# A graph layer and an eight-expert layer on one core: the last two token groups in an order of their own, and expert tiles that wait for fewer rows

## What is computed

```python
h = layernorm(x)                                   # (8, 1024, 128)
agg = eps * h + adj @ h                            # adj (8, 1024, 1024)
h = silu(rmsnorm(agg @ W1 + b1) * rms_weight)      # 512 wide
x = x + h @ W2 + b2
z = layernorm(x)
scores = z @ Wg.T + bg                             # 8 experts
top2, probs = top_k(scores, 2), softmax over the two
x = x + sum over the two: prob * (relu(z @ F1[e].T + fb1[e]) @ F2[e].T + fb2[e])
```

## Time and profile before

| | us |
|---|---|
| median of three runs | 699.27 (698.19 to 699.67) |
| the profiled execution | 698.98 |
| its span | 697.2 |
| PE busy | 591.9 (85%) |
| POOL busy | 385.1 (55%) |
| DVE busy | 453.2 (65%) |
| ACT busy | 359.3 (52%) |

### The profile page before, as it was taken

The page is one execution under the profiler, slowest core; times in us unless marked ns, Lnnn a source line. Parts: engine busy times, 40 slices in busy tenths (PEclk is TensorE's granted clock), DMA queues, the critical chain, the costliest instruction groups (busy, mean ns, idle before and its releaser), DMA issues.

```text
span 697.2 us, 13635 instructions
## 1 busy us (share of the span) xinstructions
PE 591.9 (85%) x4143; PEld 544.5 (78%) x4143; DVE 453.2 (65%) x1389; ACT 359.3 (52%) x852; POOL 385.1 (55%) x473
## 2 busy tenths in 40 slices
PE   1789899999989999999865499999999999999400
PEld 1668787878878787888754399999999999999400
DVE  2457989888898988888745345555454554555173
ACT  3257585866757586675542244444544445454200
POOL 4233268767676876767575236556555555556500
PEclk9889999999999999999995599999999999999855
DMA  7962344332444432245412655556555555563099
GB/s 262 324 184 116 121 153 148 124 111 80 147 152 153 149 114 111 90 146 153 153 39 79 205 206 191 197 183 216 181 195 195 172 204 189 185 206 126 3 398 323
DMA packets 59760, 116.49 MB, mean 167 GB/s; under 512 B 8399, under 2 KB 35072, under 8 KB 59688
## 3 DMA queue, kind: packets, MB, share of 16 engines
q1 hardware_dynamic: 50792, 98.62, 41.8%
q0 software_dynamic: 8896, 17.00, 7.2%
HBM read 61.80 MB, written 25.63 MB: 125 GB/s over the span
## 4 chain that ended last, share of the span: by engine, by line
PE 64%; DVE 12%; ACT 9%; issue 5%; DMA 4%; POOL 3%; SPq 1%; POOLq 0%; DVEq 0%; ACTq 0%
PE ps_y L628 10%; PE ps_g L628 9%; PE ps_agg L462 6%; PE ps_agg L464 5%; PE ps_agg L463 5%; PE ps_t L469 5%; PE ps_y L576 4%; PE ps_h L462 4%; PE ps_h L463 4%; PE ps_h L464 4%; DVE adjT_lo L943 3%; ACT adjT_hi L664 3%; DMA adj_in<-parts 3%; DVE hn L1026 3%; PE ps_t L605 2%
## 5 line engine op out<-in xcount | busy, mean ns | idle before, releaser
L902 POOL DMA_INDIRECT parts<-adj_in,goes x150 | 145.7, 971 | 125.7 <-ACT adj_in L781 60.1
L852 POOL DMA_INDIRECT slots<-rows,dest x128 | 128.5, 1004 | 43.5 <-issue 38.3
L781 ACT ACTIVATE adj_in<-adj_in,share 128x128 f32<-128x128 f32 x150 | 49.4, 392 | 134.8 <-issue 123.0
L943 DVE TENSOR_TENSOR adjT_lo<-ps_t,adjT_hi 128x512 fp32r<-128x512 f32 x128 | 88.1, 689 | 34.0 <-ACT adjT_hi L664 31.0
L664 ACT ACTIVATE adjT_hi<-ps_t 128x512 fp32r<-128x512 f32 x128 | 76.1, 596 | 63.5 <-PE ps_t L469 63.3
L469 PE MATMUL ps_t<-ident,adj_in 128*128 128x128 f32 x512 | 79.8, 281 | 13.2 <-POOL adj_in L838 13.2
L469 PEld LDWEIGHTS ps_t<-ident,adj_in 128*128 128x128 f32 x512 | 66.5, 146 | 31.1 <-issue 14.4
L462 PE MATMUL ps_agg<-adjT_hi,xn_hi 128*128 128x512 f32 (+1 forms) x152 | 69.9, 460 | 10.5 <-DVE adjT_lo L943 10.5
L1128 DVE CAST goes<-adj_in 128x3 int32<-128x3 f32 x50 | 9.6, 192 | 103.7 <-DMA parts<-adj_in,goes 94.3
L628 PE MATMUL ps_g<-W2e,hn 128*128 x600 | 71.0, 275 | 0.0
L628 PE MATMUL ps_y<-W2e,hb 128*128 x600 | 71.0, 275 | 0.0
(11 more groups left out here) (176 smaller groups left out, 1317.8 us busy)
## 6 DMA issues: line engine op xcount, KB each, us to landing
adj_in<-in_adj SPq DMA_DIRECT2D x16, 2048.0 KB, 10.0
W1cur<-W1e SPq DMA_DIRECT2D x26, 512.0 KB, 3.1
adj_in<-slots SPq DMA_DIRECT2D x50, 196.5 KB, 2.5
xn_hi<-W1e SPq DMA_DIRECT2D x12, 512.0 KB, 3.1
xn_lo<-W1e SPq DMA_DIRECT2D x12, 512.0 KB, 3.1
W1e<-parts SPq DMA_DIRECT2D x4, 1024.0 KB, 8.2
adj_in<-parts SPq DMA_DIRECT2D x4, 1024.0 KB, 16.0
out<-x_all SPq DMA_DIRECT2D x8, 512.0 KB, 6.2
```

The source lines that it names most:

```text
L781: ins = act.activation(ye[ku][:, j, :], yb[ku % 2][:, j, :], ACT.Copy, scale=share[ku][:, j:j + 1])
L852: pool.indirect_dma_start(out=slots, out_offset=bass.IndirectOffsetOnAxis(ap=dest[1 - par][:, c, j:j + 1], axis=0), in_=rows[1 - par][:, c ...
L902: pool.indirect_dma_start(out=parts, out_offset=bass.IndirectOffsetOnAxis(ap=goes[ku][:, j:j + 1], axis=0), in_=ye[ku][:, j, :], in_offset ...
L943: dve.tensor_tensor(adjT_lo[m % 2][:, :], ps_t[m % 2][:, :], adjT_hi[m % 2][:, :].bitcast(FP32), ALU.subtract).then_inc(s_lo, 1)
```

## The change

**Steps 0 to 15 are as before.** Behind them groups 14 and 15 (q - 1 and q, with q = 15) have a list of their own on every engine:

- PE: all four products of `first_layer` for group 15 into four banks (`h_last`), with no expert weights between them; the transposes of the hidden layer with those of group 14's normed rows (now into `ps_t[0]`) between; the second layer of group 15 with group 14's gate inside it; group 14's ranks; `expert_weights` 0 to 3; normed rows and gate of group 15; `expert_weights` 4 to 6; group 15's ranks; `expert_weights` 7. The weights now rotate over three pairs of banks (`w_bank`), so expert e waits for the copies of expert e - 2 or e - 3.
- DVE, ACT and POOL have lists that go with it. On POOL the scatter of group 13 is split around the two inverse square roots, and group 15's inverse square root stands ahead of all of group 14's scatters.
- `fill_tails` moves from SP to ACT, behind all copies of weights and ahead of ACT's first work on tiles.
- SP loads the rows of tile 0 ahead of its weights, and rows 0, 1 and 2 (`AHEAD` = 3) wait for all even groups, but for the odd groups and the paddings only up to numbers read from `enough`. DVE works those out behind `table`: if expert 0 has at least 896 + 384 t rows, then tile t lies in rows that group 15 cannot reach, and 896 (all odd groups but 15) and the 7 spare paddings are enough; if not, everything is waited for. Rows 3 wait for everything.
- DVE makes `low_weights` 5 to 7 behind the table and not within it. POOL makes three more constants at the start (`sure` and the two halves of `fewest`).

```diff
+    AHEAD = 3
+    ENOUGH = (16 * GT * (NG - 2), 16 * SPARE)
+        h_last = (ps_h[0], ps_h[1], ps_agg[0], ps_agg[1])
+
+        def w_bank(e, i):
+
+            return (ps_t, ps_agg, ps_h)[e % 3][i]
...
@@ sync
-            sp.wait_ge(s_tail, 1)
-            fill_tails(sp, range(E))
             sp.wait_ge(s_table, 1)
-            sp.wait_ge(s_wTa, 2 * E)
-            sp.wait_ge(s_wTd, E)
-            sp.wait_ge(s_fb1c, 1)
-            sp.wait_ge(s_fb2, 16)
+            sp.wait_ge(s_late, 1)
...
+                if t < AHEAD:
+                    rows_in, pads_in = [sp.value_load(enough[0:1, i, t:t + 1], min_val=ENOUGH[i], max_val=ENOUGH[i] + 128)
+                                        for i in range(2)]
+                    sp.wait_ge(s_scat[0], 16 * GT * NG)
+                    sp.wait_ge(s_scat[1], rows_in)
+                    sp.wait_ge(s_pads, pads_in)
+                elif t == AHEAD:
+                    sp.wait_ge(s_scat[1], 16 * GT * NG)
+                    sp.wait_ge(s_pads, 16 * (SPARE + E))
...
+            load_rows(0, 0)
+            sp.wait_ge(s_wTa, 2 * E)
+            sp.wait_ge(s_wTd, E)
+            sp.wait_ge(s_fb1c, 1)
+            sp.wait_ge(s_fb2, 16)
             load_weights(0, 0)
-            sp.wait_ge(s_tails, 16 * E)
-            sp.wait_ge(s_spare, 16 * SPARE)
-            sp.wait_ge(s_scat[0], 16 * GT * NG)
-            sp.wait_ge(s_scat[1], 16 * GT * NG)
-            load_rows(0, 0)
...
@@ tensor
-            first_part(pe, step, NG + 1)
+            first_part(pe, step, NG - 1)
+
+            q = NG - 1
+            pe.wait_ge(s_agg, NG)
+            first_layer(q, range(GT), h_last)
+            pe.wait_ge(s_hn, NG)
+            pe.wait_ge(s_hna, NG)
+            transpose_hidden(q, (0, 1))
+            pe.wait_ge(s_lo, TPB * NG)
+            transpose_normed(q - 1, ps_t[0])
+            transpose_hidden(q, (2, 3))
+            second_layer(q, (0,))
+            gate(q - 1)
+            second_layer(q, (1, 2, 3))
+            rank(q - 1)
+            for e in range(4):
+                expert_weights(e)
+            transpose_normed(q, ps_y)
+            gate(q)
+            for e in range(4, 7):
+                expert_weights(e)
+            rank(q)
+            expert_weights(7)
...
@@ scalar
+            for e in range(4):
+                copy_weights(e)
+            normed(q, ps_y)
+            second_rows(q)
+            for e in range(4, E):
+                copy_weights(e)
+            act.wait_ge(s_tail, 1)
+            fill_tails(act, range(E))
...
@@ gpsimd
+            scatter_rows(q - 2, 0)
+            rms_factors(q)
+            ln2_factors(q - 1)
+            scatter_rows(q - 2, 1)
+            ln2_factors(q)
+            pool.wait_ge(s_dest, q)
+            pool.wait_ge(s_row2, q)
+            for c in range(2):
+                scatter_rows(q - 1, c)
+            pool.wait_ge(s_dest, q + 1)
+            pool.wait_ge(s_row2, q + 1)
+            for c in range(2):
+                scatter_rows(q, c)
...
@@ vector
+            add_second_layer(q)
+            ln2_stats(q)
+            ln2_aggregate(q)
+            order.end()
+            order.step((NG + 2) * 22)
+            places(q - 1)
+            low_weights(0)
+            normed_rows(q)
+            for e in range(1, 4):
+                low_weights(e)
+            first_choice(q)
+            second_choice(q)
+            low_weights(4)
+            places(q)
...
+            order.link(dve.tensor_tensor(late[:, :], t_cnt[:, 0:1].broadcast_to([1, AHEAD]), sure[:, :], ALU.is_lt))
+            dve.scalar_tensor_tensor(enough[:, :, :], late[:, None, :].broadcast_to([1, 2, AHEAD]), 128.0, fewest[:, :, :],
+                                     ALU.mult, ALU.add).then_inc(s_late, 1)
+            for e in range(5, E):
+                low_weights(e)
```

More of the change, by code:

```diff
@@ new lines, in second_layer @@
+            def second_layer(q, chunks):
+                wait(pe, s_x1, q)
+                for c in chunks:
+                    pe.wait_ge(s_silu, 4 * q + c + 1)
+                    for j in range(GT):
+                        ins = pe.matmul(ps_y[:, j * P:(j + 1) * P], siluT[:, c, j * P:(j + 1) * P], W2s[:, c, :],
+                                        start=(c == 0 and j == 0), stop=(c == HC - 1 and j == GT - 1))
+                if HC - 1 in chunks:
+                    ins.then_inc(s_y, 1)
@@ new lines, in places @@
+            def places(q):
+                dve.wait_ge(s_rank, q + 1)
+                order.link(dve.tensor_tensor(place[:, :, :], ps_g[:, 0:GT * E].rearrange("p (t e) -> p t e", e=E),
+                                             base[:, None, :].broadcast_to([P, GT, E]), ALU.add))
+                dve.tensor_tensor(base[:, :], base[:, :], ps_g[:, GT * E:(GT + 1) * E], ALU.add).then_inc(s_base, 1)
+                order.link(dve.tensor_tensor(picked[:, :, :, :], onehot[:, :, :, :],
+                                             place[:, None, :, :].broadcast_to([P, 2, GT, E]), ALU.mult))
+                wait(dve, s_scat[q % 2], (q // 2) * 128)
+                with nc.allow_low_precision(reason="sums of whole numbers below 2**24, one of them not zero"):
+                    dve.tensor_reduce(dest[q % 2][:, :, :].rearrange("p c t -> p (c t)"),
+                                      picked[:, :, :, :].rearrange("p c t e -> p (c t) e"),
+                                      AX.X, ALU.add).then_inc(s_dest, 1)
@@ L1039, in step @@
-                    best(1, rest)
-                    dve.tensor_tensor(both[:, 0:GT, :], onehot[:, 0, :, :], onehot[:, 1, :, :], ALU.add).then_inc(s_both, 1)
-                    order.link(dve.tensor_tensor(rows[par][:, :, :, GAP], top[:, 1, None, :].broadcast_to([P, 2, GT]),
-                                                 top[:, 0, None, :].broadcast_to([P, 2, GT]), ALU.subtract))
-                if isinstance(g, int) and g == NG + 1:
-                    low_weights(4)
+                    second_choice(g - 2)
@@ L1055, in step @@
-                    wait(dve, s_scat[par], (q // 2) * 128 if isinstance(q, int) else (q - par) * 64)
-                    with nc.allow_low_precision(reason="sums of whole numbers below 2**24, one of them not zero"):
-                        dve.tensor_reduce(dest[par][:, :, :].rearrange("p c t -> p (c t)"),
-                                          picked[:, :, :, :].rearrange("p c t e -> p (c t) e"),
-                                          AX.X, ALU.add).then_inc(s_dest, 1)
+                    places(g - 2)
```

396 lines of the change are left out of this document (209 added, 187 removed).

## The result

| | before | after |
|---|---|---|
| median, us | 698.19 (696.96 to 699.67, five runs) | 687.58 (685.67 to 691.53, five runs) |
| the profiled execution, us | 698.98 | 691.53 |
| its span, us | 697.2 | 689.7 |

The two kernels ran side by side this time, hence a median of 698.19 for the kernel before in place of 699.27. The ratio of after to before is 0.9854, with a 95% interval of 0.9817 to 0.9891: 10.6 us less by the medians. The forecast was 691.0 against 699.27, a ratio of 0.9882, which lies within that interval.

The account below looks back on a forecast made before the run. The chain through PE from tile 0's first product, at 396.26 us, was taken as the bound; places at 371.6 plus 16.4 put it at 388.0, 8.3 less: 690.7 profiled, 691.0 median. Range 686.5 to 697.5, the forecast's own 688 to 694.

Parts of the forecast that it names:

- better: Rival: group 15's second layer ends at its fast bound, nothing lost to shared DMA engines; 687.8 us, chance 0.12.
- mark 1: Start of group 15's first layer; as a sign, anything moved before 341 us would show the forecast wrong.
- Step 1: Up to the end of group 15's second layer: 358.8 us, bounds 356.1 and 360.4, against 361.33 before.
- Step 2: Up to group 15's normed rows: 364.8 us against 369.48, with DVE's 3.93 us wait for POOL gone.
- Step 3: From normed rows to group 15's places (`dest`): 6.8 us at 2.4 GHz, against 8.15; places at 371.6.
- Step 4: From the places to tile 0's first product: 16.4 us against 18.6, including 0.5 for shared DMA engines.
- Paddings: ACT starting the eight paddings behind the places: 1.1 us each, with cover of 3 us.
- POOL's cover of 3.8 us for group 14's scatters: Ahead of tile 0's rows: group 14's scatters land at 375.2, rows 0 start at 379.0.
- PE's idle time ahead of tile 0: Sign of being right: PE's wait for tile 0's rows, 9.99 us before, would be cut.
- the clock stays low: Rival: transposes don't hold PE's clock, 1.2 GHz up to group 15's second layer and up to its places; 697.1, chance 0.18.
- The early rows don't apply: Rival: expert 0 has too few rows, so rows 0 wait for group 15's scatters; 697, chance 0.05.
- Ranks queued behind cold weights: Rival: experts 0 to 3 at 1.2 GHz, 3.6 us more ahead of group 15's transposes; 700.6, chance 0.10.

Follow-up runs that it names:

- e1: The changed kernel, but the rows of tile 0 wait for all scatters and all paddings: 694.51 us, ratio 0.9959 to the kernel before.
- e2: The kernel before with early rows and paddings on ACT, groups 14 and 15 in the old order: 699.05 us, ratio 1.0035 to the kernel before.
- e4: The changed kernel with 20 unread products filling PE's idle stretch behind group 15's first layer: 688.65 us, ratio 0.9857 to the kernel before.
- e12: The changed kernel with e9, e10, SP order rows 0, weights 0, rows 1, biases 0, and ACT's Exp table loaded before paddings: 692.55 us, ratio 0.9928.
- e3: The changed kernel with the eight paddings started by SP again, ahead of tile 0's rows: 692.46 us, ratio 0.9924 to the kernel before.
- e9: The changed kernel with `enough` made right behind the places and read once by SP, ahead of the table: 685.46 us, ratio 0.9833.
- e10: The changed kernel with group 15's ranks ahead of experts 4 to 7 and expert 4's low half made behind `enough`: 691.79 us, ratio 0.9919.
- e11: The changed kernel with tile 1's rows loaded ahead of tile 0's weights and biases: 688.45 us, ratio 0.9877 to the kernel before.

## Why the prediction was right, and where it was off

The direction, the mechanism and the range held, and e1 and e2 show the mechanism: neither half gives the gain alone. 687.58 lies 0.4 us below the forecast's own range, close to the "better" rival's number but only in part for its reasons. Between the marks the forecast was 8.3 us less, the trace shows 10.3. Step by step, from mark 1:

| step | forecast, us | measured, us |
|---|---|---|
| 1, to the end of group 15's second layer | 358.8 - 341.0 = 17.8 | 359.8 - 343.5 = 16.4 |
| 2, to its normed rows | 6.0 | 5.0 |
| 3, to the places | 6.8 | 6.9 |
| 4, to the first product | 16.4 | 16.7 |

- **Step 1 was mis-sized by 1.4 us.** "It will fall in 5 us of nothing here as well" was right: PE stood idle for 5.11 us and the clock was granted 0.50 in 352 to 354. The term for its return was too dear: I took a value between "the second layer runs slow for 3.5 us" and "no fall at all". It came back at 354.5, 0.7 us before the second layer's first product at 355.19, while PE had done nothing but transposes since 351.58. So only the transposes paid. But part of this is the luck of one execution. The kernels of the experiments other than e4 and e2 have the same list on PE up to here, and the clock came back 2.9 us behind the first transpose in after and 5.8 and 6.0 in e1 and e12, 1.5 and 1.7 us into the second layer. Step 1 took 16.4 to 16.9 us in after, e3, e9, e10 and e11, and 17.7 and 17.8 in e1 and e12, where the forecast had 17.8. In e1 the first eight products of the second layer took 1.77 us where after's took 1.06:

```profile
351.84 1.77 PE L519 MATMUL ps_y<-W2s,siluT 128*128 128x128 f32 x8
```

- **Step 2 was mis-sized by 1.0 us.** I let DVE start 0.7 us behind PE since group 14's choices might be in its way; they were, and their last step ended at 360.03, 0.2 us behind PE, so that DVE started at 360.07. The statistics and the writing of the rows took 0.3 us less each. DVE's wait of 3.93 us for POOL is gone as said.
- **Step 3 was right**: 2.4 GHz throughout, three experts' weights under the choices (ranks at 370.26, 0.25 us after `both` at 370.01). e10 shows that their place costs the places nothing that can be told.
- **Step 4 was right in sum by two errors.** Rows 1 started 8.2 us behind `enough` and not 7.5, because two register loads took 2.3 us and not 1.5; and landing took 3.15 us in place of 2.42, against 0.5 put in for shared DMA engines. In return tile 1's transposes cost 0.55 us ahead of the first product, not 1.0. e9 confirms the price of the loads by taking them out.
- **Paddings**: priced at 1.1 each, 1.04 measured; cover priced at 3 us, 3.9 measured. That this is a real edge is what e10 and e12 show, at 3.4 us and more.
- **POOL's cover of 3.8 us for group 14's scatters** was 1.4: the last of them started at 374.79 and, at 2.5 to 2.9 us, was in at about 377.5, since POOL stood for 2.02 us after the first of them. Rows 0 started at 378.99. In e9 it was gone.

The signs I gave were borne out but for two. Mark 1 moved, from 341.0 to 343.5, which I had called a sign of being wrong if it moved at all; with 338.6 to 340.5 in the other kernels it is read as spread. And PE's idle time ahead of tile 0 was to be cut, and it went from 9.99 to 10.27 us. It was a poor sign. PE's work in front of that wait ended sooner as well, so the wait moved and did not shrink.

Of the rivals, **"the clock stays low"** fell: from 354.5 to 374 the granted clock was 1.00. The rule that would have given it, in the Trainium skill's page "TensorE: Matmul & The Clock Gate", Part 4, says that transposes don't count as PE being busy as products do. The window of 354.5 to 355.0 speaks against it, with a rise to 1.00 behind transposes alone, and so does 368 to 370 with only transposes, at 1.00. e4's fall at 363, behind the same work, speaks for it, and so do e1 and e12, where the clock rose only once products ran. Taken as a rule it would have put the time at 697.1, and the measurement decides against that. (The 4.4 us that this rival put on step 3 add up to 4.6 by its own terms, 0.9 + 0.5 + 6.0 - 2.8; it changes nothing here.) Why the same row of work kept the clock in after and lost it in e4 is open.

**"The early rows don't apply"** fell with e1, which is that case made by hand: 52.3 us between the marks. **"Ranks queued behind cold weights"** did not occur in after; e4 shows it with two experts at half speed, about 1 us.

## What to carry to other kernels

When two changes both shorten one passage, price each with the other in place: here an order worth 2.9 us alone and a relaxed wait worth nothing alone made 10.3 together, because each was hidden behind what the other removed. Behind a removed wait look at the queue that issues the transfers: the first product now waits for SP's list (register loads, rows, weights, biases, register loads), and reading flags early took 2.1 us more out. Work parked on an engine "because it is idle there" has a cover in microseconds that every later reordering must be held against.

## What was not expected of the hardware

- A register load from on-chip memory is no fixed price. The six loads of `enough` in after (ns: shortest, median, longest):

```profile
L410 SPq TENSOR_LOAD <-enough x6: 263/546/855, 377.4 to 389.1; - x6
```

The long ones on the chain, at 382.07 and 383.20, stand in a window with a DMA share of 1.04; e9's load of `table` at 377.52 took 0.28 us at a share of 0.83. In e12, ACT's loads for the paddings took 0.35 to 0.94 us from 378 on, in windows at 0.68 to 1.04; in after the four of them on the chain, ahead of 376, took 0.28 to 0.35. All the long ones stand beside much traffic, but not every load beside much traffic is long (0.28 us at 0.83, 0.35 at 0.96); that the traffic is the cause was not tried by itself.
- The granted clock rose to 1.00 while PE did transposes only in after, but in e1 and e12, with the same list on PE, only when products had followed them. And filling an idle stretch moved the fall by some 15 us, from 7.6 to 22.6 us behind mark 1, and did not remove it.
- One chip ran the kernel before and four variants 15% longer, with the clock granted in full over the window shown.
